# AdaLN layer on 8 cores: where the attention read-out of each token tile stands in the order, and how the sign for rounding is taken

## The reference

```python
mod = (_silu(L0_c) @ L0_wmod).reshape(...)          # shifts, scales and gates sa, ca, ga, sb, cb, gb
h = _layernorm(x) * (1 + ca) + sa
# attention without softmax, 16 heads of 64:
q = relu(h Wq^T) / 8;  k = relu(h Wk^T) / 8;  v = h Wv^T;  u = silu(h Wu^T)
kv = sum over tokens of k^T v                       # 64 x 64 per head
out = q kv;  out = out / max(norm(out) / 8, 1e-12) * u
x = x + ga * (out Wo^T)
h = _layernorm(x) * (1 + cb) + sb
# 8-bit linear layer: weight rounded per output row, h rounded per token
w_q, w_scale = _quantize_per_channel(weight);  x_q, x_scale = _quantize_per_token(h)
x = x + gb * (x_q w_q^T * x_scale * w_scale + bias)
```

## Time and profile before

| what | us |
|---|---|
| median of 2 runs | 1279.2 (1265.51 and 1292.9) |
| the profiled execution | 1265.63 |
| its span, slowest core (core 1) | 1263.2 |
| spans of the 8 cores | 1247.1 to 1263.2 |
| PE busy | 605.8 (48% of the span) |
| DVE busy | 373.4 (30%) |
| ACT busy | 285.0 (23%) |
| POOL busy | 65.0 (5%) |

### The profile page before, as it was taken

The page is one execution under the profiler, slowest core; times in us unless marked ns, Lnnn a source line. Parts: engine busy times, 40 slices in busy tenths (PEclk is TensorE's granted clock), DMA queues, the critical chain, the costliest instruction groups (busy, mean ns, idle before and its releaser), DMA issues.

```text
span 1263.2 us, 7749 instructions; the slowest of 8 cores (1247.1 to 1263.2 us)
## 1 busy us (share of the span) xinstructions
PE 605.8 (48%) x2344; PEld 237.5 (19%) x2344; DVE 373.4 (30%) x606; ACT 285.0 (23%) x446; POOL 65.0 (5%) x68
## 2 busy tenths in 40 slices
PE   0757576049859498980033541254405532055205
PEld 0101025014324243430001200111102201022102
DVE  0000000750130300002412425455154533544552
ACT  0000000223243332320433032501233022420142
POOL 0010100010000000000000000020002000030003
PEclk9988875569979899995555755577657775577557
DMA  8486751552020000007010100021000210021001
GB/s 198 140 196 184 222 130 16 84 90 43 1 34 1 1 1 1 1 1 199 0 33 1 33 1 0 1 100 34 0 0 1 100 34 0 0 83 51 1 0 66
DMA packets 33331, 65.68 MB, mean 52 GB/s; under 512 B 2437, under 2 KB 14854, under 8 KB 33294
## 3 DMA queue, kind: packets, MB, share of 16 engines
q0 software_dynamic: 17808, 44.04, 15.0%
q1 hardware_dynamic: 15486, 21.16, 5.0%
HBM read 75.69 MB, written 8.39 MB: 67 GB/s over the span
## 4 chain that ended last, share of the span: by engine, by line
PE 43%; DVE 22%; ACT 14%; DMA 12%; issue 7%; SPq 1%; DVEq 0%; ACTq 0%; POOLq 0%; POOL 0%; PEldq 0%
PE pb L67 43%; DMA wmq<-wmod 6%; DVE h L67 3%; DVE x_fma L67 3%; DVE ouxq L67 2%; DVE M_sb L67 2%; DVE x L67 2%; DVE xq_i L67 2%; DMA bias_c<-ffn_b 2%; DMA fwS<-ffn_w 2%; ACT h L67 2%; DMA x_fmb<-x_fm 2%; ACT L67 2%; ACT sgn L67 2%; ACT o_bf L67 2%
## 5 line engine op out<-in xcount | busy, mean ns | idle before, releaser
L67 PE MATMUL pb<-wmq,silc 128*1 128x512 f32 x192 | 102.0, 693 | 82.6 <-DMA wmq<-wmod 44.1
L67 PE MATMUL pb<-ouxq,fqT 128*128 128x512 bf16 x256 | 63.8, 415 | 73.4 <-ACT ouxq L67 73.4
L67 PE MATMUL pb<-ouxq,woT 128*128 128x512 bf16 x256 | 63.3, 414 | 7.0 <-DVE ouxq L67 7.0
L67 DVE COPY mrow<-pb 1x512 f32<-1x512 f32 x12 | 8.2, 679 | 175.5 <-PE pb L67 175.5
L67 ACT ACT_TABLE_LOAD x16 | 20.5, 1283 | 163.2 <-DVE rowsB L67 38.3
L67 DVE TENSOR_REDUCE ws_c<-fwS 128x1 f32<-128x1024 f32 x8 | 9.1, 1210 | 154.0 <-DMA fwS<-ffn_w 154.0
L67 ACT ACTIVATE ouxq<-x 128x4096 bf16<-128x4096 f32 x4 | 14.5, 3618 | 172.1 <-DVE x L67 172.1
L67 PE MATMUL pb<-q_sb,kv_sb 128*128 128x512 bf16 x32 | 17.7, 554 | 72.8 <-DVE kv_sb L67 72.8
L67 PE MATMUL pb<-h1a,wqT 128*128 128x512 bf16 x128 | 33.9, 431 | 31.8 <-ACT q_sb L67 31.8
L67 PEld LDWEIGHTS pb<-wmq,silc 128*1 128x1 f32 x192 | 17.1, 92 | 166.5 <-issue 166.5
L67 PEld LDWEIGHTS pb<-ouxq,fqT 128*128 128x128 bf16 x256 | 26.6, 105 | 109.7 <-issue 85.2
(11 more groups left out here) (126 smaller groups left out, 997.8 us busy)
## 6 DMA issues: line engine op xcount, KB each, us to landing
wmq<-wmod POOLq DMA_DIRECT2D x12, 2048.0 KB, 13.5
x_fmb<-x_fm SPq DMA_DIRECT2D x8, 1024.0 KB, 5.3
out_fm<-h SPq DMA_DIRECT2D x4, 2048.0 KB, 6.9
x_tm<-x_tm POOLq DMA_DIRECT2D x4, 1024.0 KB, 10.7
x_fma<-x_fm POOLq DMA_DIRECT2D x4, 1024.0 KB, 8.3
fwS<-ffn_w SPq DMA_DIRECT2D x1, 4096.0 KB, 23.2
wqT<-wq_t POOLq DMA_DIRECT2D x1, 2048.0 KB, 31.7
wkT<-wk_t POOLq DMA_DIRECT2D x1, 2048.0 KB, 23.0
```

The source lines that it names most:

```text
L67: ins = f(*a, **kw)
```

## The change

Three edits. First, kv_sb's and rowsB's memsets, kvev and the whole of steps 1 and 2 of tile 0 (the list _b0f without its last 8 entries, which are the wom) get keys right behind the end of phase A, ahead of both weight loads in the list. Second, the read-outs of tiles 1 to 3 lose their keys and stand where the loop puts them, behind the ffm of the tile before; the wait of oev on l2m goes. Third, the sign is taken once for all 8 blocks (128x4096) from h2 before it is multiplied, into o_bf in bf16, and xqv waits for it.

```diff
+    _kvz_idx = len(sch.ops)
     sch.op("gpsimd", lambda e: e.memset(kv_sb[:], 0.0), inc=sP, event="kvz")
...
+    _kvev_idx = len(sch.ops)
     sch.op("vector", kvev, waits=[A_END, "kvz"], inc=sV, event="kv_rdy")
+    _b0f = []
...
-            _opath[i].append(len(sch.ops))
+            if i == 0:
+                _b0f.append(len(sch.ops))
             sch.op("tensor", om(), waits=w, inc=sT, event=f"{pe}_o{p}")
...
-            if p == 0 and i:
-                w.append(f"B{i-1}_l2m")
...
+            if i == 0:
+                _b0f.append(len(sch.ops))
             sch.op("tensor", wom(), waits=w, inc=sT, event=f"{pe}_wo{ec}")
...
-        _lnm_idx.append(len(sch.ops))
...
+        sch.op("scalar", lambda e: e.activation(out=o_bf[:], in_=h2[:],
+                                                func=AF.Sign),
+               waits=[f"{pe}_h2", f"{pe}_l2m"], inc=sS, event=f"{pe}_xqs")
...
-            w = [f"{pe}_qb0", f"{pe}_h2"]
+            w = [f"{pe}_qb0", f"{pe}_h2", f"{pe}_xqs"]
             sch.op("vector", xqv(), waits=w, inc=sV, event=f"{pe}_xqv{dc}")
...
-                        out=xq_i[:], in0=sgn2[:], scalar=half_c[:, 0:1],
+                        out=xq_i[:], in0=o_bf[:, dc * TT:(dc + 1) * TT],
+                        scalar=half_c[:, 0:1],
...
-            w = [f"{pe}_xqs{dc}"]
+            w = [f"{pe}_xqv{dc}", f"{pe}_xqs"]
...
-    for _i in range(1, NT):
-        for _j, _oi in enumerate(_opath[_i]):
-            sch.ops[_oi][0] = _lnm_idx[_i - 1] + 0.5 + _j * 0.001
+    _K0 = _tq_idxs[0] - 40.0
+    sch.ops[_kvz_idx][0] = _K0 - 0.3
+    sch.ops[_kvz_idx + 1][0] = _K0 - 0.2
+    sch.ops[_kvev_idx][0] = _K0 - 0.1
+    for _j, _oi in enumerate(_b0f[:-8]):
+        sch.ops[_oi][0] = _K0 + _j * 0.01
```

More of the change, by code:

```diff
@@ L737, in kvev @@
         return ins
+    _kvev_idx = len(sch.ops)
     sch.op("vector", kvev, waits=[A_END, "kvz"], inc=sV, event="kv_rdy")
+    _b0f = []
     _P_B0 = float(len(sch.ops))
-    _opath = []
-    _lnm_idx = []
     for i in range(NT):
         pe = f"B{i}"
-        _opath.append([])
         for p in range(NP):
```

## The result

The changed kernel takes **1247.5 us** (median of 7 runs, 1245.46 to 1250.67); the kernel before, over its 6 runs by then, 1266.81. The ratio is **0.9849, 95% interval 0.9834 to 0.9864**: 1.5% faster, and by more than the measurement is unsure of. The forecast was 1244, with a range of 1232 to 1260.

What follows compares the result with a forecast made beforehand. It took the kernel as bound by a serial chain of waits between engines, plus an idle wait for ffn_w. From 1265.6 us, -23.2 + 1.3 + 0.8 - 0.4 = -21.5 gave 1244, range 1232 to 1260.

Steps and rivals of the forecast that it cites:

- Edit 1 gains 23.2: Front: tile 0's read-out and norm go under the wait for ffn_w; wom starts at 678.0, not 701.18, gaining 23.2 us.
- The table load costs 1.3: Tile 0's second layernorm: its Sqrt finds another table loaded, so a load stands on the road, losing 1.3 us.
- Edit 2 gives back 55.9 and costs 56.7: Read-outs of tiles 1 to 3: 55.9 us returned between lnm and xh2m, 56.7 lost behind the ffm; net loss 0.8.
- my upper bound of 3.5: Moved read-outs of tiles 1 to 3: with all matmuls at the slow clock, the move costs +3.5 us.
- Edit 3 gains 0.4: Rounding: eight blocks save 3.85 us a tile, the first xq_i comes 3.8 later; net gain 0.4 in all.
- the hidden sign: Rival: ACT's sign hides under the maxima and small steps, 15 us less, giving 1229; chance 0.04.
- The clock stayed up: Rival: all pairs of the moved read-outs run at the fast clock, 6.9 us less, time 1237; chance 0.20.
- The front did not crawl beside the transfers: Rival denied: tile 0's copy, read-out and norm slow beside the transfers; 1269 if they take twice as long; chance 0.04.
- The copy of the sums was not held: Rival denied: an unseen wait holds the copy until ffn_w lands, the front gains nothing, time 1267; chance 0.08.
- 13.7 us from lnm to xh2m in every tile: Sign of being right: with read-outs gone from there, lnm to xh2m takes 13.7 us in every tile.
- the 2% line: Chances: a measurement tells about 2% from no change, 1240.3 us or less; the forecast's sum was called 3.4 short.
- 42.3 us moved under a cover of 23.6: Front: tile 0's copy, read-out and norm moved under the wait for ffn_w, less the delay they cause.

Runs made afterwards that it cites:

- the norm cut in two: Changed kernel, tile 0's norm split: row-sum steps stay ahead of the maxima, spreads and 16 multiplications go between the weight's transposes; 1238.3 us, ratio 0.9695 to the kernel before.
- edit 1 alone: Kernel before, with only tile 0's copy of the sums, read-out and norm put ahead of the weight's row maxima; 1246.05 us, ratio 0.9819.
- early sign: Changed kernel with the one 128x4096 sign issued on ACT right behind h2f, ahead of the Ln; 1228.76 us, ratio 0.9679 to the kernel before.
- the norm put back: Changed kernel with tile 0's norm behind the transposes again, only the copy of the sums and read-out ahead of the maxima; 1247.96 us, ratio 0.9828.
- the cover under DVE's passes: Changed kernel with early sign, shortened read-outs, and tiles 1 to 3's read-outs beside DVE's two passes over h2; 1165.08 us, ratio 0.9125 to the kernel before.
- shortened read-out: Changed kernel, four read-outs with a second buffer for squares and the next pair's matmul ahead of this pair's sum; 1212.67 us, ratio 0.9491 to the kernel before.
- edit 2 alone: Kernel before, with only the read-outs of tiles 1 to 3 moved behind the ffm of the tile before; 1273.4 us, ratio 1.0039.
- edit 3 undone: Changed kernel with the sign taken block by block behind each product again, into its own buffer; 1248.83 us, ratio 0.9831 to the kernel before.

## Why the prediction was right, point by point

1. *Edit 1 gains 23.2.* Measured 23.3 (138.01 to 114.67). That the two agree to 0.1 is luck: the 138.01 holds the transfer, and over the eight cores the gain is 20.8 to 24.8, 23.0 on average. The steps held too: norm at 592.2 on a core that ended phase A 0.3 later (591.7 predicted), maxima at 609.5 (609.1), wom at 678.55 (678.0). The reading that a delay of the maxima is passed on in full is shown by the kernel with the norm cut in two: the maxima start 10.2 us earlier (32.0 us behind the issue for 42.3), the first x2f comes 10.0 earlier.
2. *The table load costs 1.3.* The page has 17 loads, and l2ev to xh2m of tile 0 is longer by 1.46 in the kernel with edit 1 alone. The Trainium skill (ScalarE: Activation LUTs, "What ACT_TABLE_LOAD costs") gives about 2.7 us for a switch of table set, a load and a drain. The trace agrees with the load (1283 ns, the mean of 17) and shows no drain: 1.46 us was the whole cost. ACT stood idle before this load.
3. *Edit 2 gives back 55.9 and costs 56.7.* Together with the table load, l2ev to xh2m gave back 54.7 (54.6 by my terms); the new places cost 56.3. By itself the edit was 0.4% slower, about 5 us (1.9 to 8.0 by the interval), and so in the middle above my upper bound of 3.5. The read-outs themselves lie within it: 0.6 the worse on core 3 and 0.5 on average.
4. *Edit 3 gains 0.4.* It cost 0.4: in tiles 0, 2 and 3 it gained 0.07 each (16.44 to 16.37), and in tile 1 two of the eight conversions came late (17.01). The early sign showed that my account of the cause was right, the place behind the xs_sb copy, and my price of it too low: I had the hidden sign at 15 us and it was 18, because I left the product waiting for the xs_sb copy's turn, from which it was free.
5. *The rivals.* The clock stayed up into the third pair only: in the moved read-outs, matmuls of 0.38 turned to 0.59 in the third pair, as in the row I had taken. The sign was not hidden. The front did not crawl beside the transfers: 20.84 us ahead of rowsB, to the hundredth what it was without them. The copy of the sums was not held.
6. *Signs and sums that were off.* I had named 13.7 us from lnm to xh2m in every tile as a sign of being right. It is 15.25 in tile 0 and 12.3 and 12.4 in tiles 1 and 3, since lnm took 4.97 and 5.06 us and not the 6.12 of tile 3 before; wom, ahead of it, took about as much longer (16.6 us for 15.6 in tile 1), so this is no gain. In the chances, the sum is 3.8 short of the 2% line and not 3.4, which changes nothing. I had written that no engine computes in the wait for ffn_w; POOL is busy there for 0.87 us, and DVE, ACT and PE stand still.

The forecast was 3.5 us too low, and the table says where: the term "first x2f to l2ev" (+0.8, wom and lnm at a clock that rose later: in tile 2 the granted clock of this stretch is 0.70 for 0.76, and it takes 36.61 us for 34.99), the small terms of edit 3 (0.8 from what I had), the scaling behind the ffm (0.3), the small steps (0.2) and the start (0.3), against 0.5 gained on the two terms for the read-outs and the front; and the median lies 1.5 above the profiled execution's 1245.98. Over all eight cores the miss is plainer: phase B is 4.2 us longer than before (561.92 for 557.75), where my terms give 1.7. I had put the stretches of wom, lnm and ffm as unchanged, and they are 2.0 longer: 1.6 from the first x2f to l2ev and 0.4 from the last xq_i to the last ffev. None of these changes the mechanism.

Where I had weighed wrongly is the attribution, though the sum hides it: I counted edit 1 as "42.3 us moved under a cover of 23.6". The kernel with the norm put back shows that only the first 25 of these 42 us were of use.

## What to carry to other kernels

Between engines that hand work to one another, moving a piece out of an uncovered place gains at most the wait that it lies beside in its new place; so before moving it, name that wait in the timeline, and check by comparing tiles (here the last one, which had no such piece) what the old place cost. A pass that is independent of the chain is worth something only if its engine's queue lets it start early: one operation's place in the order was worth 18 us here. And a serial piece that stands uncovered can be made short (a second buffer, the next matmul ahead of this sum) before looking for a place to hide it: here the shortening took 38 us out of the four read-outs, twice what the change as a whole did, and with the early sign, the cover under DVE's passes and the cut norm the kernel came out 9% shorter.

## What the runs showed that I had not expected

- **The transfer's spread went off the road.** In the kernel before, the time from the issue of ffn_w to tile 0's first x2f was 135.47 to 139.46 us on the eight cores, as the transfer took longer or shorter; in the changed kernel it is 114.63 to 114.69 on all eight, since the maxima no longer wait for the transfer. With the norm put back behind, it differs again (113.05 to 115.74).
- **The fast clock lasted through the shortened read-out.** Behind the ffm it ran all its matmuls at 0.38 to 0.39 us (core 6, the first of three; in the second, the last one took 0.59), where the serial one fell to 0.59 in its third pair. PE idled 0.3 to 0.6 us ahead of most sums there, where it had idled 1.4; whether this is the reason was not tested.
- **Two late conversions, always at the same place.** In tile 1 the last xq_i comes 11.94 us behind the first, in place of 11.31, on every core of the changed kernel and of three more (in three others 11.67). With the old sign, tile 2 has 15.50 for 15.22 in the kernels with edit 1 or edit 2 alone, tile 1 has 15.47 in the one with edit 3 undone, and the kernel before has no late one. So it moves with the program. The traces point to the loading of instructions: on the slowest core of the changed kernel the queue "q14 instruction" moves a packet at 915.72 and one at 918.39 us, in this stretch, and none in the same stretch of the other tiles. Over all cores of all eleven kernels, each of the 80 stretches that came out late holds a packet of an instruction queue (up to 1.5 us behind its last xq_i), and of the 272 on time 56 do. That the packets are the cause is not shown.
